# GNN message passing on one core: three-bank PSUM rings, longer distances between engines, and a slot wait on each sixth gather

## The reference

```python
ew = edge_attr @ edge_w + edge_b                      # (100000, 256)
for l in range(3):
    residual = x
    msg = relu(x[src] * ew)
    out = 0
    for i in range(3):                                # three edge types
        h = segment_sum(msg * (edge_type == i), dst) * inv_cnt[i]
        out = out + h @ weights[l, i]
    x = residual + relu(out + x @ roots[l] + biases[l])
return layernorm(x_in + x)
```

## Time and profile before

| what | us |
|---|---|
| median of 3 runs (2966.05 to 2969.5) | 2969.16 |
| span of the profiled execution | 3581.6 |
| TensorE busy | 2843.8 (79%) |
| GpSimd busy | 2224.3 (62%) |
| VectorE busy | 2148.4 (60%) |
| ScalarE busy | 1289.4 (36%) |

### The profile page before, as it was taken

One profiled execution on the slowest core, in us unless ns is written; L12 is line 12 of the kernel. 1 busy time (PEld: TensorE's weight loads), 2 busy tenths in 40 slices (PEclk: granted clock), 3 DMA queues, 4 the chain that ended last, 5 costly groups with the idle time before them and its releaser, 6 DMA issues.

```text
span 3581.6 us, 59909 instructions
## 1 busy us (share of the span) xinstructions
PE 2843.8 (79%) x18436; PEld 2613.2 (73%) x18436; DVE 2148.4 (60%) x6028; ACT 1289.4 (36%) x2738; POOL 2224.3 (62%) x2364
## 2 busy tenths in 40 slices
PE   6888888888888877787777877777777777787777
PEld 6777777777777777777777777767777777776776
DVE  5666666666666555555555555555556656665665
ACT  5555555555555322222222222222222222222222
POOL 6666666666666566666666666656666666666664
PEclk9999999999999888888898889988888888899898
DMA  6554555555455444444444444444444444444443
GB/s 148 135 137 132 137 135 138 136 137 137 131 137 145 133 120 127 125 130 127 126 127 127 134 124 127 131 127 132 126 124 128 125 127 131 125 130 124 128 128 99
DMA packets 334989, 465.42 MB, mean 130 GB/s; under 512 B 158995, under 2 KB 221646, under 8 KB 334670
## 3 DMA queue, kind: packets, MB, share of 16 engines
q0 software_dynamic: 112608, 307.65, 30.1%
q1 hardware_dynamic: 221244, 153.70, 15.6%
q10 hardware_dynamic: 818, 0.18, 0.0%
HBM read 403.94 MB, written 57.36 MB: 129 GB/s over the span
## 4 chain that ended last, share of the span: by engine, by line
PE 59%; issue 17%; DVE 9%; another core or an unknown queue 8%; ACT 4%; DVEq 2%; DMA 0%; ACTq 0%
PE bank L911 29%; PE bank L867 14%; PE bank L961 12%; DVE acc L1138 4%; PE bank L846 2%; DVE xg L1300 1%; ACT oh_a L812 1%; DVE t L1155 1%; ACT at L753 1%; DVEq L1274 1%; PE bank L936 1%; DVEq L1138 1%; ACT xg L791 1%; DVE S L1097 1%
## 5 line engine op out<-in xcount | busy, mean ns | idle before, releaser
L700 POOL DMA_INDIRECT xg<-x,idx x1540 | 1457.0, 946 | 870.6 <-issue 351.7
L911 PE MATMUL bank<-S,xg 128*128 128x96 f32 x9384 | 1450.5, 304 | 360.3 <-issue 176.3
L911 PEld LDWEIGHTS bank<-S,xg 128*128 128x128 f32 x9384 | 1313.6, 216 | 429.2 <-issue 385.4
L791 ACT ACTIVATE xg<-xg 128x512 f32<-128x512 f32 x1170 | 736.7, 630 | 2102.3 <-DVE xg L1300 1193.8
L1300 DVE TENSOR_TENSOR xg<-xg,bank 128x512 f32<-128x512 f32 x1170 | 800.8, 684 | 691.0 <-remote 329.4
L1138 DVE TENSOR_TENSOR acc<-acc,bank 128x192 f32 x2346 | 816.7, 348 | 570.0 <-PE bank L911 343.0
L867 PE MATMUL bank<-wsb,at 128*128 128x256 f32 x4692 | 985.7, 337 | 213.6 <-issue 123.3
L700 POOL DMA_INDIRECT xg<-in_x_dram,idx x782 | 742.2, 949 | 454.2 <-PE bank L911 211.2
L867 PEld LDWEIGHTS bank<-wsb,at 128*128 128x128 f32 x4692 | 749.3, 214 | 297.6 <-issue 195.9
L961 PE MATMUL bank<-W,acc 128*128 128x256 f32 (+1 forms) x1764 | 515.9, 415 | 7.2 <-issue 6.4
L961 PEld LDWEIGHTS bank<-W,acc 128*128 128x128 f32 (+1 forms) x1764 | 386.9, 258 | 17.3 <-issue 12.1
(11 more groups left out here) (75 smaller groups left out, 789.7 us busy)
## 6 DMA issues: line engine op xcount, KB each, us to landing
at<-attr_t SPq DMA_DIRECT2D x390, 128.0 KB
attr_t<-at SPq DMA_DIRECT2D x195, 128.0 KB
xg<-x,idx POOLq DMA_INDIRECT x1540
xg<-in_x_dram,idx POOLq DMA_INDIRECT x782
hs<-in_edge_attr_dram SPq DMA_DIRECT2D x194, 64.0 KB
x<-t SPq DMA_DIRECT2D x96, 128.0 KB
xblk<-x SPq DMA_DIRECT2D x96, 128.0 KB
y<-t SPq DMA_DIRECT2D x94, 128.0 KB
```

The lines of the kernel that those rows point to most:

```text
L700: eng.indirect_dma_start(out=xg[:, n % XR, :], out_offset=None, in_=rows_in, in_offset=bass.IndirectOffsetOnAxis(ap=rows_at, axis=0)).then ...
L791: eng.activation(v, v, ACT.Relu).then_inc(s_r, 1)
L911: last = eng.matmul(sums_bank(l, q, i)[:, 192 * i + 96 * h:192 * i + 96 * h + 96], xg[:, n % XR, 128 * h:128 * h + 128], S[:, slot(l, 2 * ...
```

## The change

- The rings `pE` and `pA` get a third bank. TensorE makes edge weights two pairs ahead of the product instead of one, and VectorE adds the sums of pair q-3 instead of q-2. The steps of a block, its loads and its stores move by a step or two.
- The banks for this are those of the transposes. The constants `steps_of`, which the selectors are compared with, move into spare columns of the three `pA` banks, and so do the counts. The transposed node rows share the ring of the edge weights, in the order in which TensorE comes to them (`users`).
- The attributes are given to the program already turned and twice, 64 rows of 100096 (`attr_2`), and `attr_turn` and `attr_copy` are gone: ScalarE copies rows 0 to 63 to `at`, VectorE writes the low part to rows 32 to 63. The loads are 128 KB for four tiles.
- The counts of a block are copied to `kept` (49 copies) before `count` uses them.
- Of GpSimd's gathers only those with n a multiple of 6 wait, for the six slots of n to n+5.

```diff
-        pE = bank[0:2]
-        pA = bank[2:4]
+        pE = [bank[0], bank[1], bank[4]]
+        pA = [bank[2], bank[3], bank[5]]
...
+        for l in range(L):
+            for q in range(-3, end):
+                if (0 if l else -1) <= q < NP - 2:
+                    users.append(("edges", l, q + 2))
...
+                users += [("turned", l, k) for k in range(NB) if q == turn_step(k)]
+        turn_of = {u: i for i, u in enumerate(users)}
...
+        def shared_bank(what, l, i):
+
+            return pE[turn_of[what, l, i] % 3]
+
+        def free_shared_bank(eng, what, l, i):
+
+            before = turn_of[what, l, i] - 3
+            if before < 0:
+                return
+            what, l, i = users[before]
+            if what == "edges":
+                eng.wait_ge(s_m, l * NP + i + 1)
+            elif what == "turned":
+                eng.wait_ge(s_xc, NB * l + i + 1)
+            else:
+                eng.wait_ge(s_f0, NB * l + i + 1)
...
             def gather(l, j):
                 n = l * NT + j
-                if n >= XR:
-                    eng.wait_ge(s_sc, 2 * ((n - XR) // 2 + 1))
+                if n >= XR and n % 6 == 0:
+                    eng.wait_ge(s_sc, min(n - XR + 6, NT * L))
...
             def high(g):
 
-                eng.wait_ge(s_an[g % 3], attrs(g))
-                eng.activation(hs[:, g % 3, :, 0:32].bitcast(F32R), hs[:, g % 3, :, 32:64], ACT.Copy).then_inc(s_hi, 1)
...
+                eng.activation(at[0:64, g % TR, 0:w], hs[0:64, g % HR2, 0:w], ACT.Copy).then_inc(s_hi, 1)
...
-                if Q >= 2:
-                    eng.wait_ge(s_m, Q - 1)
+                free_shared_bank(eng, "edges", l, q)
...
-                if l and q == 0:
-                    eng.wait_ge(s_acc, 2 * V)
-                elif V >= 2:
-                    eng.wait_ge(s_acc, 2 * (V - 1))
+                if l and q < 3:
+                    eng.wait_ge(s_acc, NT * l)
+                elif V >= 3:
+                    eng.wait_ge(s_acc, 2 * (V - 2))
...
                 eng.wait_ge(s_xl[K % XB], 16 * (K // XB + 1))
-                if K:
-                    eng.wait_ge(s_xc, K)
...
+                free_shared_bank(eng, "turned", l, k)
...
-                        if (1 if l else 0) <= q < NP - 1:
-                            edge_weights(l, q + 1)
+                        if (0 if l else -1) <= q < NP - 2:
+                            edge_weights(l, q + 2)
...
-                        if l == 0 and q % 2 and 1 <= (q + 3) // 2 < NG:
-                            attr_turn((q + 3) // 2)
...
-                raw, high = hs[:, g % 3, :, 32:64], hs[:, g % 3, :, 0:32]
+                w = 128 * tiles_of(g)
                 eng.wait_ge(s_hi, g + 1)
-                eng.tensor_tensor(raw, raw, high, ALU.subtract).then_inc(s_lo, 1)
+                eng.tensor_tensor(at[32:64, g % TR, 0:w], hs[32:64, g % HR2, 0:w],
+                                  at[32:64, g % TR, 0:w].bitcast(F32), ALU.subtract).then_inc(s_lo, 1)
...
-                        if 0 <= q - 2 < NP:
-                            add_sums(l, q - 2, 0)
+                        if 0 <= q - 3 < NP:
+                            add_sums(l, q - 3, 0)
```

205 lines of the change are left out of this document (104 added, 101 removed).

## The result

The changed kernel takes 3159.17 us (median of 4 runs, 3155.63 to 3168.92) against 2967.91 for the kernel before: a ratio of 1.0653, 95% interval 1.0635 to 1.0671. It is slower, by 191 us. The forecast was slower by 31, with a range that ended at 3060. The direction was right, the size six times too small.

What follows compares the result with a forecast made beforehand. The prediction took GpSimd's gathers, at a 1.25 us pitch, to pace the timed kernel. It summed 2969 + 20 (shared ring) + 3 (start) + 8 (boundaries) = 3000 us, with an 8-in-10 range of 2915 to 3060.

Steps and rivals of the forecast that it cites:

- Rival A: TensorE, not GpSimd, paces the timed kernel, so removing the transposes pays: 2880 us; chance 0.20.
- 5.6. That leaves 3.1 us; no stall: Steady-state path from tile n-7's gather to its summed release: 5.6 us within 8.75 us, so no stall.
- the shared ring: Transposed nodes sharing the edge-weight banks delay two pairs' sums per block: +20 us, bounds 0 and 172.
- the attribute path: Layer 1's attribute transposes, copies, subtraction and loads: changes hidden beside the gathers, priced at 0.
- The 612 us: Profiled execution's 612.4 us over the timed median: gaps taken to belong to the profiled execution, not the timed runs.
- Transposes and loads: Layer 1: removed transposes, longer VectorE subtraction and doubled attribute loads on SyncE's queue, each worth 0 if GpSimd paces.
- Three banks, sums later: Third banks and sums taken three pairs later shorten TensorE's waits for VectorE, which GpSimd doesn't wait for: 0.
- Kept copies: The 49 added small fp32 copies on VectorE might lock GpSimd out of a shared port: at most 7 us.
- The wait of the sixth: Each sixth gather waits until tiles up to n-7 are summed, 8.75 us after tile n-7's gather started; no stall.
- Start +3 and boundaries +8: Thirteenth gather 3 us later (0 to 3.5); waits at the two layer boundaries add 8 us (5 to 9).
- C: Rival, much slower: every exposed block overruns by about 1.2 us, giving 3098 us; chance 0.08.
- D: Rival: the change doesn't do what it says and waits stay on every gather; chance none.

Runs made afterwards that it cites:

- both edits: Changed kernel with each gather waiting for its own pair's slots and the attribute store issued ahead of the load: 3017.9 us, 1.018 to the kernel before.
- own-bank kernel: Changed kernel with turned nodes and the last block's product in their own bank, edge weights in two banks, one pair ahead: 3067.4 us, 1.035 to before.
- changed kernel's second trace: The changed kernel run again unedited, beside the kernel before: 3145.6 us, 1.060 to the kernel before; the trace's span is 3146.3.
- six-slot wait with start and boundaries: Kernel before with one part of the change alone, only each sixth gather waiting, for six slots: 3006.8 us, 1.014 to the kernel before.
- Without the window: Changed kernel with one part undone, each gather waiting for its own pair's slots again: 3019.7 us, 1.018 to the kernel before.
- the twin: Kernel before with one more VectorE addition in each second pair, one input in PSUM, its result unread: 3588.2 us, 1.0005 to the kernel before.

## Why the prediction was right or wrong

**What bounds the kernel: right.** The timed kernel before is paced by the gathers: 4.29 + 2931.3 + 13.5 + 16 from the last start to the end give its 2965. TensorE is busier (88%) and yet not the bound. Rival A falls: the pitch is 1.25 at both levels, and none of the removed 131 us came off.

**The step that failed** is "5.6. That leaves 3.1 us; no stall", the path that the window of the sixth gather has to cover, and with it the two parts of the change that lengthen that path: the shared ring, at 20, and the attribute path, at 0. The window was the right place to look, and the sizes were wrong. The path measures 6.75 to 7.98 us in the kernel before and 7.66 to 9.76 in the changed one, against 8.48. Even the prediction's highest sum, 3153, lies below the measured 3159.

**The 612 us: wrong reason, right use.** They belong neither to the profile nor to the program but to the upper level. GpSimd's gaps there fall on gathers that wait for new sums (624.7 us over the 0.30 ahead of even gathers, 7.4 ahead of odd ones), so they are waits. That their sum equals the 612.4 shows only that the gathers pace that execution too; it would hold whatever makes them wait. At that level the path from a gather to its product is 9.9 us in layer 1, not landing plus a hand-over. The waits of 10.02 and 8.76 us at the boundaries belonged to it as well. At the lower level the first boundary shows 0.75, and both together have 0.6 us of excess.

**Transposes and loads: 0, wrong.** The copies and transposes were worth nothing on TensorE, as said. But the subtraction of 600 ns (682 measured) was priced as VectorE's time, and the loads, "fetched two groups ahead and hidden", without what stands behind them on SyncE's queue, the store. ScalarE waits for the store, then the relu, then the sums: with the window in place the store's lateness is worth some 40 us of waits (100.3 to 60.5). And the subtraction, with both inputs in SBUF, lengthens the gathers that start inside it, by 20 us in all in the changed kernel and by 43 where both edits stand. The two had a price of 0 and come to 58 us of excess in layer 1 together with what else that layer's attribute path does; the part of each is not fully separated.

**Three banks, sums later: 0, right** for the third bank of the sums and their later addition, as layers 2 and 3 of the own-bank kernel show. The third bank of the edge weights never ran unshared.

**Kept copies, at most 7: right.** In the changed kernel's second trace six gathers start inside one of the 49 copies, and none is lengthened. The prediction named the rule that VectorE can lock GpSimd out for these copies, and looked past the 196 subtractions. By the Trainium skill ("SBUF — State Buffer", SBUF: two separate sides) an operation with two inputs in SBUF takes the shared port pair as well, against a GpSimd operation that reads SBUF, and whichever comes second is blocked until the first ends. The gathers read their row numbers from `idx` in SBUF, and the 0.82 us above agree with that; that a subtraction behind a gather isn't held up (87 cases) does not. The Trainium skill's section "Who interferes with whom" on the same page infers that such an operation doesn't hinder the writing of a DMA's descriptors; for these indirect DMAs the 120 of 120 cases say otherwise.

**The wait of the sixth: the mechanism right, the path too short.** I had 5.6 us: 2.9 + 0.69 + 0.63 + 1.10 + 0.3. Measured in layer 2 of before: 6.75, in layer 1 7.98. The term that was mis-sized most is "0.3 for three hand-overs". TensorE takes the sums 0.75 us (layer 2) to 1.7 us (layer 1) after the relu has ended (1.38 and 2.34, less 0.63); ahead of them on its queue stand the edge weights, which wait for the same product, and at times a block's multiplication. Landing and hand-over to the product take 3.5, not 2.9. The spare is 8.48 - 6.75 = 1.7 us and not 3.1, in layer 1 0.5. So the wait binds now and then even alone: 27 times, +40 with start and boundaries where 11 was forecast.

**The shared ring: +20 forecast, 76 measured, inside its bounds of 0 to 172.** The place and the direction were right: two pairs behind each block, and the two behind those still late. I took 0.2 us for each of 98 exposed blocks from a granted clock of 0.896, as if slow stretches fell on blocks by chance. They don't: 77 of 102 begin just behind a transposition, where the shared turn makes TensorE idle. Before has 45 such stretches at the lower level (0.965), so more than half of the changed kernel's come with the change.

**Start +3 and boundaries +8:** the thirteenth gather goes at 26.30 against 20.89, 5.4 later, over its bound of 3.5, since it went earlier in before than the profile showed. Boundaries: 5.3 + 4.6 - 0.6 = 9.3, just over 5 to 9.

**The sum as measured**, from four kernels that each undo or keep a part, each against the kernel before timed beside it: six-slot wait with start and boundaries 40; shared ring 179 - 103 = 76; all the rest 103 - 40 = 63, of which 58 in layer 1. As differences of the same times they add up to 179 by themselves, and they are not independent. Without the window, layers 2 and 3 together keep 9 us over before with the ring shared, and layer 1 keeps 44.

**The chances.** C, every exposed block overrunning by 1.2 us, was the rival nearest to what happened, and had 0.08. Its price (3098) still lacked layer 1. No rival had the attribute path in it. D falls by the rows of GpSimd: inside each six the pitch stays 1.25 but for the lengthened gathers, and 102.5 of layer 1's 120.3 us of excess lie on each sixth gather. The direction was no luck: the ring, the start and the boundaries each cost time in the way that was forecast.

None of the versions beats the kernel before. It has 13.5 us over its gathers' pitch, so no order of waits can give more than that. A shorter pitch or fewer gathers could; neither was tried.

## What to carry to other kernels

Before a ring's wait is made coarser, measure the path from the trace, stage by stage and with the in-order queues on it, rather than adding up durations: here durations gave 5.6 us and the trace 6.75 to 8, against a window of 8.5. A change that lengthens the path can cost little with fine waits and much with coarse ones (layers 2 and 3 here: 9 us over before against 57), so test the two apart. For each DMA that a change moves, ask not only when it lands but which store or load stands behind it on its queue, and which engine waits for that one. Where GpSimd's gathers pace, look at VectorE's operations with both inputs in SBUF: with one input in PSUM they lengthened no gather of the twin (0 of 78).

## What the hardware showed that was not expected

- A gather that starts well inside a VectorE operation with both inputs in SBUF ends 0.82 us after that operation, in 120 of 120 cases; one that starts 0.04 before it isn't touched, and the operation isn't held up by a gather that came first (87 cases). It holds for an operation on 32 partitions as for one on 128. With one input in PSUM nothing is seen. In the kernel with both edits 196 such operations of 682 ns cost 45 us, 1.5% of its time.
- The same program takes 2965 or 3580 us, profiled or not, and one chip showed both. In the trace of before at the upper level the profiler has 612 of the 1173 semaphore updates of VectorE's products, at the lower one 1169, and updates by TensorE come 1.3 us (median) after the modelled end of their matmul, against 0.01. The excess of layers 2 and 3 there is 190 to 207 us in every kernel, with either kind of wait. What sets that level stays open.
- A single idle of 2.62 us of TensorE was followed by a stretch at a mean granted clock of 0.61, and 77 of the changed kernel's 102 stretches at the lower clock begin within 6 us of a transposition that shares the bank ring.
